# Maxima over partitions by transposes instead of GpSimd's all-reduce, with the weight preparation of the first group in another order

## What is computed

```python
xn = layernorm(x)
# retention, 16 heads of 64
q = (xn @ Wq + bq) / 8;  k = xn @ Wk + bk;  v = xn @ Wv + bv
ret = (q @ k.T) * D                       # D: causal decay, exp(decay[h] * (i - j))
ret = ret / clip(abs(ret.sum(-1)), 1, None)
g = groupnorm_per_head(ret @ v) * gn_w + gn_b
attn = (silu(xn @ Wg + bg) * g) @ Wo + bo
# linear layer, blocks of 16 rounded to e2m1 with e4m3 scales
w_ts = abs(weight).max() / (448 * 6)      # maximum over the whole weight
out = dequant(quant(xn, x_ts)) @ dequant(quant(weight, w_ts)).T * (x_ts * w_ts) + bias
return x + attn + out
```

## Time and profile before

| | |
|---|---|
| median of 3 runs | 2240.54 us (2240.36 to 2241.92) |
| the profiled execution, its own time | 2243.86 us |
| its span | 2242.0 us |
| TensorE matmul busy | 2093.9 us (93%) |
| VectorE busy | 1534.6 us (68%) |
| ScalarE busy | 686.3 us (31%) |
| GpSimd busy | 647.5 us (29%) |

### The profile page before, as it was taken

One profiled execution on the slowest core, in us unless ns is written; L12 is line 12 of the kernel. 1 busy time (PEld: TensorE's weight loads), 2 busy tenths in 40 slices (PEclk: granted clock), 3 DMA queues, 4 the chain that ended last, 5 costly groups with the idle time before them and its releaser, 6 DMA issues.

```text
span 2242.0 us, 51240 instructions
## 1 busy us (share of the span) xinstructions
PE 2093.9 (93%) x18041; PEld 1063.3 (47%) x18092; DVE 1534.6 (68%) x4375; ACT 686.3 (31%) x1318; POOL 647.5 (29%) x458
## 2 busy tenths in 40 slices
PE   3778779988899999999999999999999999999999
PEld 1334444444445455555454554554545555545444
DVE  6678769998976766666767666667676666676742
ACT  4545542222222232223222322232233222322310
POOL 1123223231323322233333222333332223333321
PEclk7889889999999999999999999999999999999999
DMA  6765633333433323233333232333332323333323
GB/s 256 255 229 199 236 99 114 108 103 95 129 117 100 107 90 98 90 103 117 113 103 103 93 99 89 104 117 113 103 104 92 101 89 103 119 109 106 100 78 122
DMA packets 180244, 269.30 MB, mean 120 GB/s; under 512 B 117184, under 2 KB 117312, under 8 KB 180160
## 3 DMA queue, kind: packets, MB, share of 16 engines
q1 hardware_dynamic: 180160, 268.19, 36.7%
HBM read 201.04 MB, written 37.75 MB: 107 GB/s over the span
## 4 chain that ended last, share of the span: by engine, by line
PE 73%; DVE 19%; issue 3%; DMA 2%; ACT 2%; SPq 1%; POOL 0%; DVEq 0%; ACTq 0%; POOLq 0%
PE mm L1188 46%; PE mm L1130 7%; PE tp L1130 6%; PE mm L1139 4%; PE tp L1198 2%; PE four L1238 2%; PE four L1251 2%; DMA ftile<-in_w_f 2%; DVE xa L772 1%; DVE xa L768 1%; DVE wo L861 1%; DVE state L961 1%; PE tp L1226 1%; DVE xa L767 1%; DVE xa L773 1%
## 5 line engine op out<-in xcount | busy, mean ns | idle before, releaser
L1188 PE MATMUL mm<-xnT,wring 128*128 128x512 f16 x6144 | 1381.9, 384 | 23.1 <-ACT gate L615 19.8
L1188 PEld LDWEIGHTS mm<-xnT,wring 128*128 128x128 f16 x6144 | 603.5, 99 | 731.3 <-issue 55.6
L646 ACT ACTIVATE work<-four,gs 128x64 f32<-128x64 f32 x512 | 158.1, 414 | 605.0 <-DVE gs L988 605.0
L505 POOL TENSOR_TENSOR yT<-gn,gate 128x512 f32 (+1 forms) x64 | 82.2, 1284 | 874.1 <-ACT gn L657 874.1
L975 DVE BATCH_NORM_STATS2 gst<-four 128x6 f32<-128x64 f32 x512 | 73.4, 215 | 215.5 <-PE four L1251 215.5
L1130 PE MATMUL mm<-wo,yT 128*128 128x512 f16 x864 | 195.4, 383 | 0.0
L488 POOL TENSOR_TENSOR qparts<-qT,qparts 128x512 f16<-128x512 f32 x64 | 83.0, 1296 | 344.5 <-ACT qT L615 344.5
L488 POOL TENSOR_TENSOR kparts<-kT,kparts 128x512 f16<-128x512 f32 x64 | 82.6, 1291 | 263.6 <-ACT kT L615 255.2
L1130 PE MATMUL tp<-wo,yT 128*128 128x512 f16 x672 | 149.6, 379 | 0.0
L1130 PEld LDWEIGHTS mm<-wo,yT 128*128 (+1 forms) x864 | 82.5, 99 | 99.7 <-issue 3.7
L615 ACT ACTIVATE vT<-mm,consts,down 128x512 f32<-128x512 f32 x64 | 49.8, 779 | 231.5 <-PE mm L1188 231.5
(11 more groups left out here) (188 smaller groups left out, 2700.2 us busy)
## 6 DMA issues: line engine op xcount, KB each, us to landing
wring<-parts SPq DMA_DIRECT2D x252, 512.0 KB, 3.5
xt<-in_x SPq DMA_DIRECT2D x34, 512.0 KB, 3.6
out<-res SPq DMA_DIRECT2D x32, 512.0 KB, 3.0
parts<-wo SPq DMA_DIRECT2D x28, 512.0 KB, 7.0
res<-in_x SPq DMA_DIRECT2D x28, 512.0 KB, 3.6
ftile<-in_w_f SPq DMA_DIRECT2D x16, 512.0 KB, 4.6
parts<-wring SPq DMA_DIRECT2D x8, 512.0 KB, 6.2
probs<-in_x SPq DMA_DIRECT2D x5, 512.0 KB, 3.8
```

The source lines that it names most:

```text
L505: nc.gpsimd.tensor_tensor(hi, gn[:], gate[:, u], ALU.mult)
L646: last = nc.scalar.activation(work[:, c * P + h * HD:c * P + (h + 1) * HD], ao[h][:, c * VW:c * VW + HD], ACT.Identity, bias=gs[:, 1, g:g ...
L1188: last = MM(mm[n % 2][:], wring[:, n, wj, k, :], xnT[:, parity, xj, k, :], start=(j == 0), stop=(j == 3 * KT - 1))
```

## The change

- The first maximum is made without GpSimd: VectorE copies each of the five columns over 128 columns (`spread`), TensorE transposes the five blocks (`turned`), VectorE reduces each to its maximum, ahead of the variances of x. The second one likewise with one column (`f_row`, `f_max_turned`), in tile 3.
- SP: `load_raw(1, c)` stands ahead of `store_parts(0, c)`; the raw slices 4 to 7 of batch 1 stand ahead of the copies and stores of tile 0; `load_slice(0, 3)` and, in tiles 1 to 3, `pass_on(0..3)` stand ahead of `move_x`, which waits for both quantized halves.
- ScalarE in the first group has an order of its own (`first_group`): squares are made up to a tile earlier, and `split_hi` is cut up: in tiles 1 to 3 slices 0, 1 stand ahead of `evacuate(0, 2)`, slices 2, 3 ahead of `evacuate(0, 3)`, slices 4 to 7 behind it.
- VectorE in the first group: `scale_batch` and six low halves stand between the two quantized halves in tiles 1 to 3; in tile 0 `mask_scores(0)` and `scale_batch` do. In tile 3 `weight_scales` moves in there too.
- TensorE: the sums stand behind `project(0, 1)` in tiles 1 to 3 and ahead of `scores(0)` in tile 0.

```diff
         # SP, body of FIRST
                     for n in range(2):
+                        if i == 0:
+                            load_raw(1, 4 + n)
                         load_slice(0, n)
-                        if i == 0:
-                            store_parts(0, 4 + n)
-                            load_raw(1, 4 + n)
+                    if i == 0:
+                        load_raw(1, 6)
+                        load_raw(1, 7)
                     next_f()
                     load_slice(0, 2)
+                    if i == 0:
+                        for c in range(4, SLICES):
+                            store_parts(0, c)
                     move_x_parts()
+                    load_slice(0, 3)
+                    if i > 0:
+                        pass_on(range(0, 4))
                     w("xq_ready", 1)
                     move_x()
                     load_x(1)
-                    load_slice(0, 3)
                     if i == 0:
-                        for n in (2, 3):
-                            store_parts(0, 4 + n)
-                            load_raw(1, 4 + n)
-                    pass_on(range(0, 4))
+                        pass_on(range(0, 4))
                     load_slice(1, 0)
                     load_slice(1, 1)
                     next_f()
...
             for c in range(4):
+                load_raw(1, c)
                 store_parts(0, c)
-                load_raw(1, c)
...
-            pool.wait_ge(row_max, 1)
-            nc.gpsimd.partition_all_reduce(alls[:, EXTRA:FMAX], maxs[:, EXTRA:FMAX], P, RMAX).then_inc(all_max, 1)
...
-                if phase == FIRST and i == CH - 1:
-                    pool.wait_ge(s["f_max"], at("f_max", SECOND, 0, 0))
-                    nc.gpsimd.partition_all_reduce(alls[:, FMAX:FMAX + KT], maxs[:, FMAX:FMAX + KT],
-                                                   P, RMAX).then_inc(all_max, 1)
...
+                    if b == 1 and c >= 4:
+                        act.wait_ge(s["w_" + MATS[c - 4]], 16)
...
+            def first_group(evacuate, affine, x_hi, copy_v, decay_k, normalize, i):
+
+                hi = lambda *slices: split_hi(i + 1, slices)
+                if i == 1:
+                    square(2, range(0, SLICES))
+                evacuate(0, 0)
+                evacuate(0, 1)
+                if i:
+                    affine(1, 1)
+                x_hi()
+                if i:
+                    hi(0, 1)
+                evacuate(0, 2)
+                copy_v(0)
+                decay_k(0)
+                if i:
+                    hi(2, 3)
+                else:
+                    square(1, range(0, 4))
+                evacuate(0, 3)
+                if i:
+                    hi(4, 5, 6, 7)
+                else:
+                    square(1, range(4, SLICES))
+                evacuate(1, 0)
+                evacuate(1, 1)
+                decay_k(1)
+                if i == 0:
+                    hi(0, 1, 2, 3)
+                evacuate(1, 2)
+                copy_v(1)
+                if i == 0:
+                    hi(4, 5, 6, 7)
+                elif i + 2 < BATCHES:
+                    square(i + 2, range(0, 4))
+                normalize(0)
+                evacuate(1, 3)
+                affine(0)
+                if 0 < i < BATCHES - 2:
+                    square(i + 2, range(4, SLICES))
+                normalize(1)
...
+            V.tensor_copy(spread.rearrange("p (j x) -> p j x", x=P),
+                          maxs[:, EXTRA:FMAX].unsqueeze(2).broadcast_to([P, NEXTRA, P])).then_inc(row_max, 1)
...
+            dve.wait_ge(row_turned, 1)
+            then(V.tensor_reduce(alls[:, EXTRA:FMAX], turned.rearrange("p (j x) -> p j x", x=P), AX_X, ALU.max))
...
+                if phase == FIRST:
+                    if i == CH - 1:
+                        spread_f_max()
+                    w("x_loaded", 0)
+                    layernorm(xt[:])
+                    w("xn_ready", 1)
+                    quantize_scales(xt, x_ts, x_r6)
+                    w("xq_moved", 0)
+                    quantize_half(xt, 0)
+                    if i == CH - 1:
+                        in_scales(weight_scales)
+                    if i:
+                        scale_batch()
+                        split_lo(i + 1, range(0, 6))
+                    mask_scores(0)
+                    if i == 0:
+                        scale_batch()
+                    quantize_half(xt, 1)
+                    if i:
+                        split_lo(i + 1, range(6, SLICES))
+                    states(0)
+                    find_f_max()
+                    if i == 0:
+                        split_lo(1, range(0, 4))
+                    group_norm(0)
+                    find_f_max()
+                    if i == 0:
+                        split_lo(1, range(4, 6))
+                    mask_scores(1)
+                    states(1)
+                    if i == 0:
+                        split_lo(1, range(6, SLICES))
+                    group_norm(1)
+                    find_f_max()
...
+            pe.wait_ge(row_max, 1)
+            for j in range(NEXTRA):
+                last = nc.tensor.transpose(turned[:, j * P:(j + 1) * P], spread[:, j * P:(j + 1) * P], ident)
+            last.then_inc(row_turned, 1)
...
                 project(0, 0)
                 project(0, 1)
+                if phase == FIRST and i:
+                    w("normed", 0)
+                    if i == CH - 1:
+                        pe.wait_ge(f_spread, 1)
+                        nc.tensor.transpose(f_max_turned, f_row[:], ident).then_inc(f_turned, 1)
+                    sum_slices(i + 1, 0, SLICES)
...
                 project(1, 0)
-                scores(0)
-                project(1, 1)
                 if phase == FIRST and i == 0:
                     pe.wait_ge(sums_read, 2)
                     sum_slices(1, 0, SLICES)
+                scores(0)
+                project(1, 1)
```

More of the change, by code:

```diff
@@ L164, in build @@
         ones = sb("ones", [P, P])
+        f_row = sb("f_row", [P, P])
         dmask = sb("dmask", [P, HEADS, SUB])
@@ L236, in build @@
         row_max = ctx.enter_context(nc.semaphore("row_max"))
-        all_max = ctx.enter_context(nc.semaphore("all_max"))
+        row_turned = ctx.enter_context(nc.semaphore("row_turned"))
+        f_spread = ctx.enter_context(nc.semaphore("f_spread"))
+        f_turned = ctx.enter_context(nc.semaphore("f_turned"))
         scales = ctx.enter_context(nc.semaphore("scales"))
@@ L258, in halves @@
             return wo[:, :, c, :]
+        NEXTRA = FMAX - EXTRA
+        spread = gate[:].rearrange("p a b -> p (a b)")[:, 0:NEXTRA * P]
+        turned = four[:, 0:2].rearrange("p b x -> p (b x)")[:, 0:NEXTRA * P]
+        f_max_turned = ao[0][:, CH * VW:CH * VW + P]
         slice_sums = ao[0][:, GROUP - SLICES:GROUP]
@@ L663, in body @@
                     return
[L664 to L667, removed]
+                if phase == FIRST:
+                    first_group(evacuate, affine, x_hi, copy_v, decay_k, normalize, i)
+                    return
                 evacuate(0, 0)
                 evacuate(0, 1)
-                if not first:
-                    affine(1, 1)
+                affine(1, 1)
                 x_hi()
-                if later:
-                    square(i + 1, range(4, SLICES))
                 evacuate(0, 2)
@@ L677, in body @@
                 decay_k(0)
-                if later:
-                    split_hi(i + 1, range(0, 4))
                 evacuate(0, 3)
-                if first:
-                    square(1, range(0, SLICES))
                 evacuate(1, 0)
@@ L685, in body @@
                 decay_k(1)
[L686 to L689, removed]
                 evacuate(1, 2)
@@ L871, in _ @@
                                        apply_absolute_value=True)
-            last.then_inc(row_max, 1)
+            then(last)
+            V.tensor_copy(spread.rearrange("p (j x) -> p j x", x=P),
+                          maxs[:, EXTRA:FMAX].unsqueeze(2).broadcast_to([P, NEXTRA, P])).then_inc(row_max, 1)
             V.memset(ones[:], 1.0).then_inc(ones_set, 1)
@@ L909, in _, with spread_f_max @@
             assert here["n"] == PER["step"][START], ("start", here["n"])
+            def spread_f_max():
+                in_scales(lambda: then(V.tensor_reduce(w_ts, maxs[:, FMAX:FMAX + KT], AX_X, ALU.max)))
+                V.tensor_copy(f_row[:], w_ts.broadcast_to([P, P])).then_inc(f_spread, 1)
             def weight_scales():
-                dve.wait_ge(all_max, 2)
-                then(V.tensor_reduce(w_ts, alls[:, FMAX:FMAX + KT], AX_X, ALU.max))
+                dve.wait_ge(f_turned, 1)
+                dve.wait_ge(summed, BATCHES + 1)
+                then(V.tensor_reduce(w_ts, f_max_turned, AX_X, ALU.max))
                 then(V.tensor_scalar(w_ts, w_ts, 1.0 / (F8_MAX * F4_MAX), None, ALU.mult))
@@ L1011, in f_scales @@
                     w("xqf_moved", j)
```

(22 more changed lines are left out.)

9 lines of the change are left out of this document (3 added, 6 removed).

## The result

The changed kernel takes 2232.64 us (median of 6, 2229.96 to 2235.42) against 2240.94 us (6 runs, 2239.40 to 2242.88) in the same comparison: ratio 0.9963, 95% interval 0.9950 to 0.9976. It is faster by 8.3 us, 0.37%. The forecast was 22 us and 2218, with 2231 as the upper end, so the time lies just outside the range.

The account below looks back on a forecast made before the run. TensorE bounds the kernel from 620 us, VectorE the second group; slack lies before 334.7 us. Terms -2 and -20.5 took the 2242.0 span to 2219.5, or 2218 as the time forecast; range 2204 to 2231.

Parts of the forecast that it names:

- Start, 8.5 us earlier: Start stage: without the GpSimd maximum, scales reach ScalarE and the first projection starts 8.5 us earlier, bias-sum collision included.
- Tile 0 gives nearly all of it back: Tile 0: waits for a copy and FFN slices leave only about 2 of the 8.5 us, bounds 0 to 8.
- scale_batch ahead of half 1, signal 18.4 in: Tiles 1 to 3: scales reach ScalarE 18.4 us into VectorE's body instead of 26.2, 7.8 us earlier.
- Signal to GroupNorm 25.0, with TensorE standing before project(1, 0): Tiles 1 to 3: scales' signal to GroupNorm takes 25.0 us against 25.1, with a TensorE stand of some 4.7 us.
- From GroupNorm to the next body +1.2 in tiles 1 and 2: Tiles 1 and 2: this stretch grows 1.2 us, from a later project(1, 3) and squares ahead of normalize(0).
- Tile 3, -7.3: Tile 3 of the first group: 7.3 us shorter, kept from a worked-out -7.5.
- The sum by profiled spans: Whole kernel: -2 up to tile 0 and -20.5 in tiles 1 to 3, -22.5 on the span of 2242.0.
- the single difference of 3.3 us: Whole kernel: the profiled execution before lay 3.3 us above its runs' median; the same difference was assumed after.
- most of it is eaten: Rival, about 2231: half 0 stays stretched, TensorE slow twice a tile, 3 to 4 us a tile left; chance 0.22.
- more comes through: Rival, about 2206: the start counts in full because FFN slices land early, and the clock stays high; chance 0.18.

Follow-up runs that it names:

- start_only: The kernel before with only the first maximum made by spread, transposes and reduction, orders and second maximum as before; 2232.55 us, -7.9 against before.
- order_only: The change with the first maximum put back on GpSimd, the second still on transposes; 2238.02 us, -2.5 against the kernel before.
- same_requests: The change with a second buffer for the raw FFN slices, each slice requested at its old place on SP; 2234.78 us, -5.3 against before.
- two_ffn_buffers: The change with raw FFN slices going in turn into two buffers, each requested one place earlier; 2210.23 us, -30.3 against the kernel before.
- start_and_buffers: start_only with the edit of two_ffn_buffers, all orders old; 2229.22 us, -11.0 against the kernel before.
- buffers_half1_slice3: two_ffn_buffers with, in tile 0, half 1 quantized ahead of mask_scores(0) and load_slice(0, 3) ahead of four stores and move_x_parts; 2205.80 us, -34.3 against before.
- buffers_slice3: two_ffn_buffers with load_slice(0, 3) ahead of the four stores and move_x_parts on SP in tile 0; 2208.84 us, -31.3 against before.
- old_tile0: The change with the old order in tile 0 on SP, ScalarE, VectorE and TensorE; 2225.43 us, -15.1 against the kernel before.

## Why the prediction was wrong, point by point

- *Start, 8.5 us earlier.* Held: 7.6. The collision with the bias sum came as worked out (signal 26.8, forecast 26.0). Of the 0.9 us that are missing, the transposes of x on TensorE account for most: they ran from 16.6 to 22.9, 6.3 us, where they took 5.0 before, and the forecast left their length unchanged. That the GpSimd maximum cost the 20.6 us around it is shown by its removal (mask done at 12.0 instead of 30.6, and 7.9 us less in start_only) and by its return in order_only. The Trainium skill's GPSIMD Engine Reference, section 2.1 (Instruction dispatch), gives about 6 us for such a first call, by which this part would have given nothing; the measurement decides against that. In start_only, where the first call of the program comes only in tile 3, 5.63 us of "issue" stand before it, as the page has it, and 8.93 behind it; what makes it 10 to 12 us in the start stage is open.
- *Tile 0 gives nearly all of it back.* Held, in each step: square(1, 7) at 69.9 ("near 70"), sums at 71.2 (70.4), the second FFN slice at 104.7 (103.8), body 1 at 126.9 (126.5).
- *scale_batch ahead of half 1, signal 18.4 in.* Held: 18.4 in tile 1 (145.22 less 126.86). Half 0 ended 16.45 in (16.6).
- *Signal to GroupNorm 25.0, with TensorE standing before project(1, 0).* Held: 24.2 in tile 1, the stand 4.1 us (4.7), the projection behind it 6.67 us. VectorE's own work, called just hidden, ended with TensorE's chain: the f maximum at 169.4, the last matmuls before GroupNorm at 169.3.
- *"From GroupNorm to the next body +1.2 in tiles 1 and 2".* **This step failed.** It was 24.9 us in tile 1, so +7.2. The profile shows VectorE standing 4.7 and 1.3 us for FFN slices; in tile 2 it stands 3.7. The forecast worked out the request and landing of the FFN slices for tile 0 and stopped there, so it put this wait at nothing in tiles 1 and 2 without a reason. There SP's transfers start with an x_lo that comes 9.9 us later in the body, with a move_x that took 3.97 us to issue (1.23 before) among them, while VectorE wants the slice 7.2 us earlier. same_requests, two_ffn_buffers and start_and_buffers show that the late request is what costs: no change from the buffer alone, 22 us from the earlier request in the new order, at most a few in the old. With the slices in time tiles 1 and 2 take 63.7 and 62.4 us, against 62.5 and 61.4 forecast: of the 8.1 us that they fell short, 6 come back, and 2 stay unexplained.
- *Tile 3, -7.3.* Held: -6.8. It has no FFN slice, and its body is 62.5 us against 69.3.
- *The sum by profiled spans.* -22.5 forecast, -13.1 measured: tile 1 fell short by 4.9 us and tile 2 by 3.2, the rest by 1.3 in all. The medians differ by 4.8 less than the spans. The profiled execution of the kernel before took 2.9 us more than its median of 2240.94, that of the change 1.6 less than its own; 0.3 lie between span and time. The forecast carried over the single difference of 3.3 us to the changed kernel and had no width for it; this part is chance, not an effect of the change.

The rival "most of it is eaten" (2231) had the time nearly right and the main cause wrong: half 0 did not stay stretched (4.2 us in tile 1). Its other condition, TensorE slow twice a tile, was met in part: in tile 2 the projections took 7.56 us for 24 matmuls at 215.3 and 12.30 for 48 at 253.8, where 5.34 and 10.52 are their usual times. The rival "more comes through" (2206) had its condition, FFN slices in time, made true by two_ffn_buffers, and that took 2210.

## What to carry to other kernels

When an edit moves work inside one engine's order, go through every single-buffered transfer that the moved work consumes, in every iteration and not only in the first: where is its request in the DMA queue now, what stands ahead of it, and what does VectorE or TensorE do until it lands. Here 22 us of waits were removed (29.2 to 7.6) and bought about 7 until one more request was moved forward, and then some 19. And a second buffer was worth nothing as long as the request stayed where it was (-5.3 against -5.7).

The best kernel of the study (buffers_half1_slice3, 2205.8 us) beats the kernel before by 34.3 us (1.5%).

## What the runs showed of the hardware that was not expected

- After a single 2.3 us stand of TensorE the distance between two profiles of the same kernel grew from 0.3 to 4.1 us, with the granted clock at 0.83 in the 10 us around the stand. All six profiles with that stand have a rest 2.5 to 6 us longer than the seven without.
- A partition_all_reduce of 0.4 us on GpSimd had 10.2 and 11.6 us of "issue" before it in the start stage and 5.6 to 5.9 in tile 3; the next GpSimd instruction came 8.4 to 9.1 us after it.
- The issue of one transposed move on SP (L345, 16-bit, 128 x 1024) took 3.97 and 3.81 us in tiles 1 and 2 of the change, where two transposed moves and nine 512 KB transfers had been issued ahead of it without a pause, and 1.24 in tiles 0 and 3; in the kernel before it took 1.23 in all four. In tiles 1 and 2 of the other runs of the new order, with such transfers ahead of it, it took from 1.57 us (buffers_slice3, tile 1) to 6.36 (old_tile0, tile 2).
- In the first group a 512 KB FFN slice was read 9.4 us after its request (171.08 to 180.5), against medians of 3.5 and 3.6 us from issue to landing over the whole span for the weight slices and the tiles of x, of the same size.
